# Loads of x moved from SyncE's DMA queue to ScalarE's, in a fused AdaLN adapter and quantised feed-forward kernel

## The reference

```
w_down = down_project * (cond @ down_gamma) + cond @ down_beta      # per batch item, 256 x 64
w_up   = up_project   * (cond @ up_gamma)   + cond @ up_beta        # 64 x 256
y      = relu(x @ w_down) @ w_up + x
h      = bitlinear(y, w1, b1)        # 256 -> 1024
h      = gelu(h)
out    = x + bitlinear(h, w2, b2)    # 1024 -> 256

bitlinear(x, w, b): x' = x * rsqrt(mean(x^2) + eps)
                    xq = x' rounded to 127 levels of its row's largest value
                    wq = w rounded to -1, 0, 1 times mean(|w|)
                    xq @ wq^T + b
```

## Time and profile before

| | |
|---|---|
| time, 3 runs | 107.11 us median, 105.73 to 107.49 |
| span of the profiled execution | 103.5 us (its own whole time is not among the views; the median is 3.6 us above the span) |
| busy in the span | PE 67%, DVE 65%, ACT 61%, POOL 47% |
| DMA | 9.16 MB, of which 6.98 MB read from HBM, nearly all before 24 us |
| queue q1 (SyncE's loads and stores) | 3030 packets |
| queue q10 (ScalarE's two b1 loads) | 12 packets |

### The profile page before, as it was taken

One profiled execution on the slowest core, in us unless ns is written; L12 is line 12 of the kernel. 1 busy time (PEld: TensorE's weight loads), 2 busy tenths in 40 slices (PEclk: granted clock), 3 DMA queues, 4 the chain that ended last, 5 costly groups with the idle time before them and its releaser, 6 DMA issues.

```text
span 103.5 us, 1853 instructions
## 1 busy us (share of the span) xinstructions
PE 69.8 (67%) x481; PEld 41.4 (40%) x488; DVE 67.8 (65%) x129; ACT 62.7 (61%) x123; POOL 48.5 (47%) x117
## 2 busy tenths in 40 slices
PE   0494193395799807993993997599369469665570
PEld 0331160231534404573462645457245355563450
DVE  5154467934387999529929965992980990996720
ACT  0400452376398973994988599499589569770210
POOL 5058057216115567268167546917826744505000
PEclk9999555558999999999999999999999999999998
DMA  2779999920000000000200200020020020011022
GB/s 64 252 235 380 406 395 438 418 111 0 0 0 6 0 9 0 0 0 0 101 0 0 101 0 0 0 101 0 0 101 6 0 101 0 0 59 43 0 108 101
DMA packets 3048, 9.16 MB, mean 88 GB/s; under 512 B 345, under 2 KB 601, under 8 KB 2530
## 3 DMA queue, kind: packets, MB, share of 16 engines
q1 hardware_dynamic: 3030, 9.06, 23.2%
q10 hardware_dynamic: 12, 0.02, 0.1%
HBM read 6.98 MB, written 2.10 MB: 88 GB/s over the span
## 4 chain that ended last, share of the span: by engine, by line
issue 24%; PE 20%; POOL 16%; ACT 12%; DVE 12%; DMA 8%; POOLq 1%; DVEq 1%; SPq 1%; ACTq 1%
DMA w<-w_t 8%; POOL rms L669 7%; PE q2t_ps L302 4%; PE out_ps L313 3%; PE q1t_ps L275 3%; ACT junk L402 3%; ACT q1t L417 3%; PE h L288 3%; DVE m L564 2%; DVE q L527 2%; POOL top L675 2%; POOL step L679 2%; DVE mx L534 2%; POOL var L666 2%; ACT junk_y L410 2%
## 5 line engine op out<-in xcount | busy, mean ns | idle before, releaser
L394 ACT ACTIVATE g<-h,deq 128x1024 f32<-128x1024 f32 (+1 forms) x16 | 17.7, 1112 | 3.0 <-PE h L295 1.4
L425 ACT ACTIVATE q2t<-q2t_ps 128x512 f32<-128x512 f32 x16 | 9.6, 600 | 16.0 <-PE q2t_ps L302 16.0
L534 DVE TENSOR_REDUCE mx<-g 128x1 f32<-128x1024 f32 (+1 forms) x16 | 18.8, 1208 | 0.0
L288 PE MATMUL h<-w1q,q1t 128*128 128x512 f16 x64 | 17.8, 404 | 0.7 <-ACT q1t L417 0.7
L402 ACT ACTIVATE junk<-g 128x1024 bf16<-128x1024 f32 (+1 forms) x16 | 16.9, 1054 | 0.0
L313 PE MATMUL out_ps<-w2q,q2t 128*128 128x256 f16 x128 | 16.2, 272 | 0.0
L666 POOL TENSOR_SCALAR var<-ms 128x4 f32<-128x4 f32 (+1 forms) x10 | 2.6, 263 | 26.7 <-ACT junk L402 18.9
L275 PE MATMUL q1t_ps<-ident,q 128*128 128x128 f16 x32 | 3.3, 228 | 15.8 <-issue 11.6
L302 PE MATMUL q2t_ps<-ident,q 128*128 128x128 f16 x128 | 9.8, 219 | 5.6 <-ACT q2t L425 3.1
L313 PEld LDWEIGHTS out_ps<-w2q,q2t 128*128 128x128 f16 x128 | 12.5, 98 | 2.1
L560 DVE RECIPROCAL scale<-step 128x4 f32<-128x4 f32 (+1 forms) x10 | 1.7, 173 | 17.3 <-POOL step L679 17.3
(11 more groups left out here) (80 smaller groups left out, 109.6 us busy)
## 6 DMA issues: line engine op xcount, KB each, us to landing
w<-w_t SPq DMA_DIRECT2D x2, 1024.0 KB, 10.0
out<-x SPq DMA_DIRECT2D x8, 256.0 KB, 2.0
xd<-x_dim SPq DMA_DIRECT2D x1, 1024.0 KB, 13.5
x<-x_tok SPq DMA_DIRECT2D x1, 1024.0 KB, 15.5
xd<-x_dim SPq DMA_DIRECT2D x2, 256.0 KB, 6.2
x<-x_tok SPq DMA_DIRECT2D x2, 256.0 KB, 7.9
xd<-x_dim SPq DMA_DIRECT2D x1, 512.0 KB, 12.1
x<-x_tok SPq DMA_DIRECT2D x1, 512.0 KB, 12.0
```

The lines of the kernel that those rows point to most:

```text
L288: pe.matmul(h_ps[s][:, cols], q1t[:, s, c, :], w1q[:, c, cols], start=(c == 0), stop=False)
L394: a.activation(g[:, j, s, :], h_ps[s][:, :], ACT.Gelu, scale=deq[:, j, SLOTS + s:SLOTS + s + 1])\
L425: a.activation(q2t[:, s].rearrange("p k t -> p (k t)").bitcast(F32), q2t_flat, ACT.Copy)\
L534: v.tensor_reduce(mx[:, j + 2, s:s + 1], g[:, j, s, :], AX.X, ALU.max, apply_absolute_value=True)\
```

## The change

The eight loads of x and xd leave SyncE's block. ScalarE issues groups 0 and 1 first of all, without a wait, then the wait on `b1_zero` and its two b1 loads, then groups 2 and 3, then its table load. SyncE issues dpk, upk, its b1 load, w1, w2 and b2 back to back. Semaphores, tiles and arithmetic are the same.

```diff
         @block.sync
         def _(sp):
-            def load_group(n):
-                at, count, _ = GROUPS[n]
-                sp.dma_start(xd[:, at:at + count], x_dim[:, at:at + count]).then_inc(xd_in[n], 16)
-                sp.dma_start(x[:, at:at + count], x_tok[:, at:at + count]).then_inc(x_in[n], 16)
-
             sp.dma_start(dpk[:], down_pack).then_inc(dpk_in, 16)
             sp.dma_start(upk[:], up_pack).then_inc(upk_in, 16)
             sp.wait_ge(b1_zero, 1)
             sp.dma_start(b1f[64:67, :], b1_rows).then_inc(b1_in, 16)
-            load_group(0)
             sp.dma_start(w1[:], w1_t).then_inc(w1_in, 16)
-            load_group(1)
             sp.dma_start(w2[:], w2_t).then_inc(w2_in, 16)
-            load_group(2)
             sp.dma_start(b2[:], b2_rows).then_inc(b2_in, 16)
-            load_group(3)
...
         @block.scalar
         def _(a):
+            def load_group(n):
+                at, count, _ = GROUPS[n]
+                a.dma_start(xd[:, at:at + count], x_dim[:, at:at + count]).then_inc(xd_in[n], 16)
+                a.dma_start(x[:, at:at + count], x_tok[:, at:at + count]).then_inc(x_in[n], 16)
+
+            load_group(0)
+            load_group(1)
             a.wait_ge(b1_zero, 1)
             for b in range(2):
                 a.dma_start(b1f[32 * b:32 * b + 3, :], b1_rows).then_inc(b1_in, 16)
+            load_group(2)
+            load_group(3)
             a.preload_act_table(ACT.Gelu)
```

## The result

The changed kernel took 109.17 us (108.49 to 109.98, 4 runs) beside 106.42 us (105.72 to 107.49, 4 runs) of the kernel before: ratio 1.0365, 95% interval 1.0234 to 1.0497. It is slower. The forecast was 110.8 us, range 107.0 to 113.2.

What follows compares the result with a forecast made beforehand. The prediction took POOL's chain, started after w1 landed, as the bound, with b1 having 3.9 us of slack. Late b1 added 3.7 us to the 103.5 us span, other terms 0 or hidden; plus 3.6 gave 110.8 us, range 107.0 to 113.2.

Steps and rivals of the forecast that it cites:

- The bound and its slack: POOL at the head: chain starts at 13.98 us; b1 work ends at 10.09, so b1 may land 3.9 us later.
- The term that decided: Last b1 load, behind 3.71 MB, lands at 13.6 us; POOL's chain starts at 17.7: +3.7 us, bounds +2.5 and +6.0.
- The subtraction itself: POOL's preparation of b1 was taken to last 3.85 us, as in the profile of the kernel before.
- w1: w1 load: more x bytes ahead, +0.66 us, landing at 12.5 us and chain at 14.6, hidden behind late b1.
- upk, y of pair 0 and the table load: Head: upk lands by 6.4 us, y ends at 11.75, ACT's table load ends at 7.3; all hidden, 0.
- The clock at the head: TensorE's 1.2 GHz stretch moves with pair 0's first-layer matmuls: 0, though up to 1.8 us either way.
- The sum: Whole kernel: span 103.5 + 3.7 = 107.2 us, plus 3.6 us between span and median, 110.8 us.
- A: Loads served in order of issue, both b1 loads ahead of w2: w1's +1.3 us counts, 108.4 us; chance 0.11.
- the b1 case: Late b1 loads delay POOL's first chain: 110.8 us, own range 108.8 to 113.2; chance 0.66.
- B: Queues share by bytes: b1 hidden at about 9.5 us, w1 2.6 us later, 109.7 us; chance 0.05.
- D: The queue makes no difference, only issue time is saved: 107.1 us; chance 0.11.
- C: Not slower: second queue fills the idle stretch at 2 to 7 us, b1 and w1 not held up: 105.7 us; chance 0.07.

Runs made afterwards that it cites:

- The two later profiles: The kernel before, no edit, profiled a second and third time: 106.00 and 105.79 us, one run each.
- the kernel with b1 first: Changed kernel with ScalarE's two b1 loads issued ahead of its four early x loads: 111.11 us beside 105.48, ratio 1.0601.
- b1 ahead of w1 on SyncE: Changed kernel with ScalarE's two b1 loads issued from SyncE ahead of w1: 107.47 us beside 105.94, ratio 1.0162; again 106.54 beside 105.85, ratio 1.016.
- b1 between the groups: Changed kernel with ScalarE's two b1 loads moved between x groups 0 and 1: 105.89 us beside 105.85, ratio 1.0067.
- b1 late alone: Kernel before, all loads on SyncE, ScalarE's two b1 loads moved there behind w1: 109.0 us beside 105.94; single later run 107.55 beside 105.48.
- b1 work behind the first chain: Changed kernel with POOL's two b1 subtractions moved from before(-3) to before(-1): 106.67 us beside 105.94, ratio 1.0054.

## Why the prediction was right

**The bound and its slack: right.** b1's slack was read as 3.9 us, the end of its work against the start of the chain. The two later profiles give 3.4 to 3.5. POOL got the loads 5.7 us later than in those two, the work took 0.5 us longer, and the chain started 2.8 us late: what was over.

**The term that decided, +3.7 us: right mechanism, too large.** It measured 2.8 us. The subtraction began at 11.69 us, not 13.8, below even the low bound of 12.6. The 3.71 MB ahead of the last b1 load came close (3.62 MB had moved at 11.6 us), but the clock time at which the stream reaches them was read from the stream of before: 13.6 us. In the changed kernel the stream reached 3.71 MB at 11.85 us, 1.75 us earlier. The prediction had that gain as a bound of 0.57 us and took 0. That is the step that failed, and the bound too was low by its own rows: it priced the stretch by the busy share (0.62), while the bytes in it (165 of 395 GB/s) make 0.87 us of 1.5, and the neighbouring stretches were not looked at (3.7 to 4.75 us: 274 GB/s before, 405 after; 6.25 to 7.5: 288 and 411). That the bytes came out so near is partly luck: w2, counted whole among them, landed only at 14.7 us, so they were not the bytes that the prediction counted. The round robin of the Trainium skill (DMA: Bandwidth & Descriptors, Queues, rings and completion order) fits in that neither queue went ahead of the other alone; but xd of group 0, issued 0.5 us behind w1 in the kernel with b1 first, landed 1.7 us after it with a quarter of the bytes, which is closer to order of issue. Against strict order stands that the same xd, issued 0.1 us behind w2, landed 1.5 us before it, and that in the changed kernel's second profile x of group 1, issued 0.2 us ahead of w1, landed 2.1 us after it (at 13.4 us). No run settles the rule.

**The subtraction itself**: 4.39 us instead of 3.85, and in the second profile 3.85, where var took 0.66 instead of 0.22; both together took 4.6 and 4.5 us. **The chain's own length**: top was 0.5 us shorter in both, which wasn't in the sum.

**w1: wrong sign.** 12.5 us was forecast, 10.95 and 11.3 measured. That the filled idle stretch paid for the bytes ahead of it fits the stretches above, but no run separates the two. It didn't count, being hidden behind b1, as foreseen.

**upk, y of pair 0 and the table load: right.** upk at 5.9 us (bounds 5.1 and 6.4; 6 to 6.4 was named as the sign), y ended at 11.3 (11.75), table load ended at 6.95 (7.3).

**The clock at the head: right.** The first layer ran at the lower level in both.

**The sum: in range, 1.6 us too high.** The 3.6 us between span and median only lead back to the median of before, 107.1 us, so that the forecast is 107.1 + 3.7. Measured by the medians it is 106.4 + 2.75: 0.95 us of the error is the term, 0.7 the base, whose three runs came out high. The 3.6 is no cost of an execution: four runs of the changed kernel have time minus span at 1.8 to 1.9.

**The rivals.** A (108.4 us) came nearer in time than the b1 case. Its condition was not met, since SyncE issued w2 at 2.72 us, between ScalarE's two b1 loads (2.63 and 3.4 us), and its 2.7 MB had moved by 9.4 us, not at b1's landing; but b1 did land 3 us before w2, as A has it. B fell: w1 landed earlier, not 2.6 us later. That the time stays (D) fell; what decides is the order of ScalarE's own loads more than the queue. The rule of the Trainium skill (DMA: Bandwidth & Descriptors, Issuing engines are not separate DMA queues), that only issue time is saved, falls short here: from 4.75 to 6.25 us the seven profiles with x on ScalarE's queue moved 262 to 414 GB/s, the five with all of x on SyncE's 115 to 209. A second queue alone does not do it, though: with b1 first on ScalarE's queue 2.14 MB had moved at 9.5 us, as with one queue (2.07 to 2.19), against 2.73 to 2.77 in the six others. C was half right: the stretch was filled and w1 came earlier, but b1 was held up.

**Open:** a smaller cost of the two queues themselves is not excluded. In all seven sets of runs with x on ScalarE's queue the time is further above before than the transposes of pair 2 are late in the profile: by 0.1 to 1.0 us in the medians, 0.5 to 1.7 by the ratios. So b1 ahead of w1 on SyncE came out 1.6% above before with a head only 0.5 us late, and the twelve runs with b1 between the groups show nothing of the 1.0 us gained at the head. One profile stands for a whole set of runs there, so it can be chance; no run tests it. Open too is how late b1 was in the slowest runs with b1 late alone, which have no profile. Executions of one kernel differ by 1.2 to 4.6 us here, which hides a microsecond.

## What to carry to other kernels

When loads move to another queue, look at what was already on it, small loads above all, and at the whole program of the engine that waits for them: a 12 KB load can hold the longest chain. A load's place in its queue and its moment of issue, which changed together here, decide behind which megabyte it waits: the b1 loads issued at 1.96 us behind two x transfers landed at 7.3 us, those issued at 2.63 us behind four at 11.7. The head of a DMA stream is not fixed when its order changes; price an idle stretch in it by the bytes it moved, and not by the busy share alone. Before adding up to a time, take a second profile of the kernel before: one execution can be an exception in more than one place.

## What the runs showed of the hardware

With one queue, the 16 DMA engines stood partly idle between 4.75 and 6.25 us though transfers issued more than a microsecond earlier were outstanding; busy 0.50 to 0.87 of their time in five profiles. With the four early x transfers first on a second queue they were busy 1.04 to 1.13 of it (five profiles); with b1 among or ahead of them 0.87 and 0.79. The cause of the idle stretch was not looked for. Within one queue a later small load can land first: with b1 late alone, the b1 loads issued right behind w1 landed at 10.66 us in one profile, w1 at 11.1, and at 11.46 us in the other, w1 at 11.1.

TensorE's granted clock fell to 1.2 GHz between 38 and 42.5 us in eleven of twelve profiles, within or up to 1.3 us behind a stretch in which PE stood idle for 3.4 to 3.7 us, and stayed there for 3.4 or 6.8 us. The twelfth, the first of before, has the same idle stretch (3.42 us) and keeps the full clock. From the transposes of pair 2 to those of pair 4 the lower clock costs 0 to 1.2 us. It fell once more between 76 and 91 us in five profiles. In three of these (the first of the changed kernel, b1 first, b1 work behind the first chain) it was low again before the end, and from the transposes of the last pair to the end they need 22.9 us, the nine others 20.5 to 20.8. All three have x on ScalarE's queue; four others with it don't have this, so nothing ties it to the change.

In two profiles (the second of the changed kernel, and b1 first) the clock row shows full speed up to 41 and 42 us, and their mean granted clocks (0.96 and 0.94) say nothing of the first layer, whose matmuls took as long as at 1.2 GHz in the others:

```profile
22.61 1.89 PE L279 MATMUL h<-w1q,q1t 128*128 128x512 f16 x4 [0.69 <-ACT q1t L417]
```
